# A fused two-stage attention kernel: the first key tile's exponentials move into the ring, the second stage's ring gets 12 places, and the planner's steps are replaced

## The reference

```python
x = x + tanh(g_xattn[0]) * xattn(layernorm(x), ctx_768, ...)   # softmax(q k^T / 8) v, 8 heads of 64; @ Wo + bo
x = x + tanh(g_ffn[0]) * ffn(layernorm(x), ...)
# ffn: q = (q / |q| + query_embedding) * softplus(temperature); softmax(q k^T / sqrt(32)) v, 16 heads of 32
#      gates = softmax(h @ Wr.T + br), top 3 of 15, times softmax(h @ Ws.T + bs); out = h * sum(gates) @ Wp.T + bp
```

## Time and profile before

| | us |
|---|---|
| median of 3 runs | 4596.27 (4593.71 to 4602.74) |
| profiled execution | 4595.59 |
| its span in the trace | 4593.8 |
| PE busy (matmuls) | 4350.3, 95% of the span |
| POOL busy | 3338.4, 73% |
| DVE busy | 2881.1, 63% |
| ACT busy | 2528.2, 55% |
| PE weight loads | 2348.5, 51% |

### The profile page before, as it was taken

How to read it: one execution, slowest core, us unless ns; L and a number is a source line. 1 busy time by engine, 2 the same in 40 slices (tenths; PEclk the granted TensorE clock), 3 DMA queues, 4 the chain that set the end, 5 groups by cost and what they waited for, 6 DMA issues and landing times.

```text
span 4593.8 us, 67810 instructions
## 1 busy us (share of the span) xinstructions
PE 4350.3 (95%) x21568; PEld 2348.5 (51%) x21568; DVE 2881.1 (63%) x3955; ACT 2528.2 (55%) x4641; POOL 3338.4 (73%) x2667
## 2 busy tenths in 40 slices
PE   4899999999999999999999999999999999999997
PEld 3455555555555555554445444544454454544443
DVE  4455656464646464676777767676777667677661
ACT  2353535454535454546666666567557666565664
POOL 1566666767666667558888878778788879677897
PEclk7899999999999999999999999999999999999999
DMA  7476766666656666653435345354443454362532
GB/s 230 129 194 173 205 173 197 178 194 182 182 168 184 174 177 175 169 147 104 136 106 173 90 136 154 83 155 117 124 143 103 124 152 106 112 181 70 146 109 83
DMA packets 516175, 682.26 MB, mean 149 GB/s; under 512 B 42736, under 2 KB 371952, under 8 KB 506608
## 3 DMA queue, kind: packets, MB, share of 16 engines
q1 hardware_dynamic: 515824, 677.92, 52.7%
HBM read 323.57 MB, written 150.99 MB: 103 GB/s over the span
## 4 chain that ended last, share of the span: by engine, by line
PE 80%; issue 8%; ACT 4%; DVE 4%; POOL 2%; DMA 2%; SPq 0%; ACTq 0%; POOLq 0%; DVEq 0%
PE aux L957 28%; PE aux L1049 19%; PE aux L1063 18%; PE aux L1031 7%; PE aux L1075 4%; DVE nm L1404 2%; ACT probs L1247 2%; PE aux L1001 1%; POOL added_f L936 1%; PE aux L1083 1%; PE aux L977 1%; POOL added L936 1%; ACT more L1247 1%; DMA xs<-in_x 1%; DMA v_kept<-v_out 0%
## 5 line engine op out<-in xcount | busy, mean ns | idle before, releaser
L936 POOL TENSOR_TENSOR added<-added,probs 128x512 f32<-128x512 f32 x1433 | 1792.0, 1289 | 773.7 <-PE aux L1063 620.7
L1404 DVE TENSOR_REDUCE nm<-aux 128x2 f32<-128x1024 f32 x1536 | 1810.9, 1220 | 581.9 <-PE aux L1031 581.4
L1247 ACT ACTIVATE probs<-aux 128x512 f32<-128x512 f32 x2151 | 1172.3, 603 | 876.1 <-PE aux L1049 740.0
L1049 PE MATMUL aux<-stack 128*128 128x512 f32 x4096 | 1323.0, 427 | 76.5 <-ACT probs L1247 36.5
L1049 PEld LDWEIGHTS aux<-stack 128*128 128x128 f32 x4096 | 711.4, 189 | 740.7 <-issue 284.0
L1063 PE MATMUL aux<-probs,v 128*32 128x512 f32 (+1 forms) x4302 | 934.5, 610 | 4.3 <-ACT probs L1247 2.3
L936 POOL TENSOR_TENSOR added_f<-added_f,probs 128x512 f32<-128x512 f32 x537 | 672.3, 1287 | 119.6 <-PE aux L1063 73.8
L957 PE MATMUL aux<-xT_hi,wqk 128*128 128x512 f32 x1536 | 560.4, 404 | 1.0 <-ACT more L1247 0.6
L1031 PE MATMUL aux<-ck_hi,cq_hi 32*128 32x512 f32 (+1 forms) x3072 | 453.9, 483 | 53.3 <-DVE nm L1404 35.8
L1031 PEld LDWEIGHTS aux<-ck_hi,cq_hi 32*128 32x128 f32 (+1 forms) x3072 | 181.0, 185 | 512.4 <-issue 511.0
L957 PE MATMUL aux<-wvo,parts 128*128 128x512 f32 x1536 | 400.2, 403 | 10.6 <-issue 10.2
(11 more groups left out here) (132 smaller groups left out, 4387.4 us busy)
## 6 DMA issues: line engine op xcount, KB each, us to landing
wqk<-w_split SPq DMA_DIRECT2D x256, 256.0 KB, 3.8
wvo<-w_split SPq DMA_DIRECT2D x64, 1024.0 KB, 7.2
parts<-h_kept SPq DMA_DIRECT2D x128, 512.0 KB, 3.9
stack<-cq_hi SPq DMA_DIRECT2D x128, 256.0 KB, 5.2
stack<-ck_hi SPq DMA_DIRECT2D x128, 256.0 KB, 5.5
v_kept<-v_out SPq DMA_DIRECT2D x128, 256.0 KB, 2.3
v<-v_kept SPq DMA_DIRECT2D x64, 512.0 KB, 4.4
h_kept<-h_hi SPq DMA_DIRECT2D x128, 256.0 KB, 2.8
```

What stands on the lines that cost most here:

```text
L936: pool.tensor_tensor(onto, onto, exp_buffer(T, e), ALU.add).then_inc(added_ok, 1)
L1049: ins = pe.matmul(out, stack[:, g % 2, e * ph.SLOTS + ks, jt * P:(jt + 1) * P], stack[:, g % 2, e * ph.SLOTS + qs, n * HALF:(n + 1) * HALF ...
L1247: act.activation(exp_buffer(T, e), aux[:, o.bank["S", T, e], :], ACT.Exp, scale=ph.SCALE).then_inc(probs_ok, 1)
L1404: dve.tensor_reduce(nm[:, half, first:first + 2 * TT - t:TT], aux[:, b:b + 2, :], axis=AX.X, op=ALU.max, negate=True).then_inc(emptied["dv ...
```

## The change

Four edits that go together.

- **First key tile.** All 8 key tiles of a half go through the ring. The sums get their own function, `sum_buffer`, on the same memory `added` and `added_f`. POOL's first addition of a half reads two exponentials (tiles 0 and 1) and writes the sum; it no longer waits for `PV`, but for the `sm` that read this sum buffer two halves ago. A ring place of tile 0 is free when tile 1 has been added (`added_by`). `ex` of tile 0, which waited for an `sm` two halves back, waits now as the other tiles do.
- **Ring.** The second stage's ring has 12 places (7 in `probs`, 5 in `more`); the first stage's stays at 7.
- **Memory.** The room comes from two buffers: the squares of the queries go into the place of the queries' low parts (`squares(n)`, one for each half, so that ACT waits for the copies of the group before it writes them), and the output bias of both stages lies in one tile `bo`, which a transfer `bi` and a scaling `bm` fill again between the stages.
- **Plan.** All numbers of `AT` are new, those of the second stage too, and the dependencies follow the edits above.

```diff
-        self.NP = 10 if ffn else 7
+        self.NP = 12 if ffn else 7
...
     def ring(self, T, e):
 
         t = T - TURN * self.first
-        return (t - t // TT - 1) * self.G + e
+        return t * self.G + e
 
     def ring_prior(self, T, e):
 
         m = self.ring(T, e) - self.NP
-        if T % TT == 0 or m < 0:
+        if m < 0:
             return None
         s, head = divmod(m, self.G)
-        return s + s // (TT - 1) + 1 + TURN * self.first, head
+        return s + TURN * self.first, head
+
+    def added_by(self, T, e):
+
+        return self.adds(T + (T % TT == 0), e)
...
-      dict(p=[3.46, 20.78, 34.23, 52.32], over=5.91, held=0.03, mx0=-6.14, mxn=10.85, ...
+      dict(p=[1.05, 21.66, 33.04, 50.6], over=5.54, held=0.1, mx0=-6.28, mxn=10.98, ...
...
+        self.add(("bi", 0), "sp", TURN * B + 50, [("xb", TT * B - 1)])
+        self.add(("bm", 0), "dve", TURN * B + 54, [("bi", 0)])
...
-            if T % TT == 0:
-                i = T // TT % 2 * ph.G + e
-                return added[:, i, :] if i < 4 else added_f[:, i - 4, :]
             i = ph.ring(T, e) % ph.NP
             return probs[:, i, :] if i < X.NP else more[:, i - X.NP, :]
 
+        def sum_buffer(h, e):
+
+            i = h % 2 * stage(h // HALVES).G + e
+            return added[:, i, :] if i < 4 else added_f[:, i - 4, :]
+
+        def squares(n):
+
+            return cq["lo"][:, n * HALF:(n + 1) * HALF].bitcast(F32)
...
                         if T % TT == 1:
-
-                            pool.wait_ge(weighed, T)
+                            if h >= 2:
+
+                                wait_full(pool, ("sm", h - 2), *([("sm", h - 1)] if h == HALVES * B else []))
+                            first = exp_buffer(T - 1, e)
                         else:
 
                             pool.wait_ge(added_ok, ph.adds(T - 1, e))
-                        pool.tensor_tensor(onto, onto, exp_buffer(T, e), ALU.add).then_inc(added_ok, 1)
+                            first = onto
+                        pool.tensor_tensor(onto, first, exp_buffer(T, e), ALU.add).then_inc(added_ok, 1)
...
-                        if (g, n) > (NG * B, 0):
-
-                            wait_emptied(act, ("ss", g, 0) if n else ("ss", g - 1, 1))
-                        act.activation(sq[:], src, ACT.Square, bias=bq[:, g % NG:g % NG + 1]).then_inc(sq_ok, 1)
+                        if n == 0:
+                            wait_stacked(act, g - 1, range(stage((g - 1) // NG).G))
+                        act.activation(squares(n), src, ACT.Square, bias=bq[:, g % NG:g % NG + 1]).then_inc(sq_ok, 1)
...
                             act.wait_ge(weighed, last + 1)
-                            if ph.is_added(last):
-                                act.wait_ge(added_ok, ph.adds(last, head))
+                            if last % TT < TT - ph.APART:
+                                act.wait_ge(added_ok, ph.added_by(last, head))
```

More of the change, by code:

```diff
@@ L577, in attention @@
         ones = sb("ones", [P, X.SUM])
-        bo_x = sb("bo_x", [P, DM])
+        bo = sb("bo", [P, DM])
         tg = sb("tg", [P, 2])
@@ L1000, in _ @@
                         pe.wait_ge(sq_ok, q_at["pqa", g, n])
-                        done(it, pe.matmul(out, blk[:], sq[:], start=True, stop=True))
+                        done(it, pe.matmul(out, blk[:], squares(n), start=True, stop=True))
                     elif kind == "vp":
@@ L1071, in _ @@
                         pe.wait_ge(added_ok, ph.adds(end - 1 - ph.APART, G - 1))
[L1072 to L1073 removed]
+                        if ph.APART:
+                            pe.wait_ge(probs_ok, ph.scores(end - 1, G - 1))
+                        for i in range(1 + ph.APART):
                             for e in range(G):
[L1075 removed]
+                                term = exp_buffer(end - i, e) if i else sum_buffer(h, e)
+                                ins = pe.matmul(out[e * D:(e + 1) * D, :], ones[:, 0:ph.SUM], term, start=i == 0, stop=i == ph.APART)
                         done(it, ins)
```

66 lines of the change are left out of this document (32 added, 34 removed), and 4 rows, old and new, of the table TAKES.

## The result

The kernel after takes 4469.32 us (median of 4 runs, 4468.38 to 4470.65), the kernel before beside it 4597.48 us. The ratio is 0.9726, with an interval of 0.9714 to 0.9737: 2.7% faster, 128 us.

A forecast was written before the change was run, and what follows sets the result against it. The prediction took the second stage to alternate between stretches bound by PE and by POOL, with too few buffers to average them. Terms -59 - 8 - 5 + 0 - 4 = -76 us from 4595.6 gave 4519 us, range 4480 to 4588.

The forecast's parts named there:

- PE has 0.5 us more to do than its busy mean: Second stage: PE's work in a batch is 303.4 us after the change, against a busy mean of 302.9 before.
- an idle time of 5.1: Batches 9 to 14: PE's idle time left in a batch, from 2.4, 1.7 and 1.0 us, giving batches of 308.5.
- the prices are 2.5% low: Batch 12 before: 294.4 us of PE's work counted against 301.8 busy, so counts were multiplied by 1.03.
- The rival called the floor: Rival, chance 0.13: POOL's earlier start removes nearly all PE idle time and matmuls flow without gaps; -115, 4480 us.
- The bound of 4471: Whole kernel, limit from below: all of PE's second-stage idle time and 10 us at the start go, 125 us.
- a half can't be shorter than that for long: Second stage: POOL's 24 additions of 1.29 us, 31.0 us, limit a half however little PE has to do.
- The rule that the prediction cites: Whole kernel: rule against the forecast; relieve the engine with highest occupancy, POOL, whose work doesn't change, so no gain.
- That wait goes: Second stage: POOL's first addition no longer waits for `PV`, so POOL enters each half up to 2.9 us earlier.
- 2.6 us that the ring lends: Middle of a second-stage half: with 12 places instead of 10, POOL may be 2.6 us later without being felt.
- POOL as the bound all along: Rival, chance 0.08: POOL's work is unchanged, so a wait removed on it turns into another; 4595 to 4600 us.
- The loss at the start of a half: Rival 'Slower', chance 0.09: the first tile's exponentials wait at a half's start; +62 or +31, 4627 us.
- Waits for ACT in the fourth half: Rival 'Half of the gain', chance 0.15: idle time returns as waits for ACT, bunched in the fourth half; 4560 us.

The follow-up runs named there:

- ring11: The kernel after with 11 places instead of 12 in the second stage, sequence planned anew for 11: 4580.71 us, ratio 0.9973.
- light additions: POOL's second-stage additions of key tiles 2 to 6 on half of the columns: 4573.13 us in the kernel before, 4461.03 us in the kernel after.
- old_steps1: The kernel after with the first stage's planner steps (first dict of AT) from before: 4600.39 us, ratio 1.0018.
- both light engines: Exponentials (batches 9 to 15) and POOL's second-stage additions, key tiles 2 and later, on half of the columns: 4548.93 us in before, 4446.42 us in after.
- old_steps: The kernel after with both dicts of AT from before, so the new structure with an order planned from the old steps: 4612.77 us, ratio 1.0039.

## Why the prediction was wrong in size

**The mechanism, as far as it held.** PE's work is spread by the new order as counted, the light halves go but for the fifth, and batches 9 to 14 are alike. That the spread is what brings the gain did not hold as I wrote it: ring11 is as even by the count and takes 320.8 us a batch, and the new steps with 10 places are more even than before and slower. The prediction took the evenness from after's finished order, and what else that order does right came with it unnamed: it leaves PE 19 gaps in a batch, where before has 42 on average and ring11 32 to 34 in batches 12 and 13. The halves of batch 12 come out at 40.8, 36.6, 35.6, 36.6, 29.5, 45.6, 34.1 and 45.0 us, for counts of 36.8, 37.9, 35.3, 36.5, 25.9, 43.7, 33.1 and 44.8. The first stage stayed at its time, with 236.2 to 236.5 us in five of batches 1 to 6. Batch 5 takes 240.8, which is over the bound of 238 that I set; light additions in after show such a batch at another place (batch 4), so it doesn't belong to the order.

**The step that failed: PE's busy time was taken as its work.** The prediction said "PE has 0.5 us more to do than its busy mean", 303.4 us in a batch; that is why even an idle time of 5.1 gave only 308.5. With 1,652 matmuls in batch 12 of either kernel, the busy time fell to 296.7, and to 296.8 in the mean of three. This term alone is 6 x 6.6 = 40 us too high. Idle time was forecast at 5.1 and is 7.0, 6 x 1.9 = 11 us the other way; the two make 28 to 29 of the 29.4 us by which batches 9 to 14 miss. What lies in the 6.1 us between the busy means 302.9 and 296.8 can be worked out from the list of matmuls. PE has 36, 41 and 48 gaps in batches 12 to 14 before (idle times of any length) and 19, 19 and 18 after. In before the matmul after a gap adds 0.50 us of busy time on average, where the same kinds add 0.33 in the flow; in after it is 0.52 and 0.38. That makes 41.7 x 0.17 - 18.7 x 0.14 = 4.5 us. Another 1.1 is the granted clock, below; 0.5 stays unexplained. So by this estimate a gap costs its idle time and 0.15 to 0.2 us that the profile books as busy. The counts had shown it: busy time lies 7.4, 8.6 and 11.8 us over the count in batches 12 to 14 before, with 36, 41 and 48 gaps, and 2.7 in after with 19. The prediction read the first three as "the prices are 2.5% low" and carried them over as work. The Trainium skill, Perfetto Trace Analysis, section Identifying the Most-Contended Engine, says that matmul busy time is no good measure of how close PE is to its limit, since pipelined matmuls look smaller in the trace. I had quoted the first half of this and then added up busy time all the same. The trace agrees that busy time is not work, though here it is larger than the counted work, and larger the more gaps there are. The rival called the floor had this mechanism ("matmuls that now wait between exponentials flow without gaps") and its 4480 is the nearest of my times; I gave it 0.13. The bound of 4471 from "PE's idle time only" was no bound.

**The step that was wrong without showing in the sum: POOL as the pace.** I wrote that "a half can't be shorter than that for long", 31.0 us, and took POOL's being busy in each of 31.4 us as the proof. With POOL's additions light the half takes 30.6. Nor are 31.0 us a floor for a half: the half of `old_steps1` above takes 26.1 with whole additions, and the profile of the kernel before has one of 29.7, the fifth of batch 13, which the prediction does not use. POOL was busy all the time because the half was about as long as its work for other reasons too: by the timeline, round trips of score and exponential with nothing of PE's between them. The rule that the prediction cites, from the Trainium skill, Perfetto Trace Analysis, section Identifying the Most-Contended Engine (relieve the engine with the highest occupancy, PE judged by its weight loads), would have pointed to POOL and is no better: halving most of its additions gains 0.4%. What fits is the section Optimization Strategy of that page of the Trainium skill, on kernels with several regimes, which may gain when these are interleaved; the new order does that, though ring11, as even by the count, gains nothing in batches 9 to 14. The same section of the Trainium skill takes repeated gaps on the engine that should be busy as a possible lack of buffers. Here two more places without the order gave nothing (4636 against 4632 us), and one less with it cost 93.

**The terms for the first addition and for the ring.** "That wait goes" was right, the 68.8 us of the earlier trace rows are gone. That it frees POOL by 2.9 us in a half was not: POOL now waits for exponentials instead (28.8 + 28.6 + 14.7 + 14.4 = 86.5 us in the two rows of after above and the two for `more`; 47.8 in before), and is waited for only 0.8 us. The ring's "2.6 us that the ring lends" to POOL had the wrong borrower, the lead of the scores. No step of my sum said that the order depends on 12 places, where 11 cost 81 of the 88 us.

**Smaller terms.** Batch 7 gave 10.6 us where I took 0: the first stage was counted only for its steady batches, and in batch 7 PE has 27 matmuls less in the new order, some 4 us at my prices; its busy time falls by 7.4 and its idle time by 3.3. Batch 0 gave 5.2 us although PE has 19 matmuls more there, some 3.4 us: idle time falls from 16.4 to 9.1 us and the loss by the clock (below) from 11.9 to 5.1. The start (-2.1 against -4) was nearly right. Batch 8 (-8.9 against -8) was right by luck: its terms (321.3 less 17.9 idle, plus 1.5 of work) reach "about 313" only with 8 us left idle that I gave no reason for; 12.7 were idle, and the busy time was 3.7 lower where 1.5 more had been counted. Batch 15 with the tail (-10.1 against -5) was too low; its idle time is 31.7 us against 38.6. Light additions gain 13 us in before's batch 15, so POOL is felt there, where I took nothing for it. These and the 29.4 us make the miss: 29.4 + 10.6 + 5.2 + 5.1 + 0.9 - 1.9 - 0.5 = 48.8 us, against the profiled execution.

**The other rivals.** POOL as the bound all along is refuted by its light additions. The loss at the start of a half did not come, though POOL has little room: with the wait for `PV` kept the kernel loses 338 us. Waits for ACT in the fourth half are small: it takes 36.6 us, and 35.8 with exponentials and additions light, where the prediction had 1.0 for them.

**What stays open.** Of before's light half of 31.4 us, 25.6 are counted; both light engines together took 1.9. That the remaining 3.9 are gaps for want of PE's other work is argued from the timeline; no run filled them. What in after's order leaves PE so few gaps is known only in part: the count of work by halves does not tell it, and DVE's maxima close together are one likely cost of the other orders. Before's own order with the new buffers wasn't tried (the kernel `old_steps` has an order planned anew), nor more than 12 places. Of the runs with the whole computation none is faster than the kernel after.

## What to carry to other kernels

An engine that is busy for all of a stretch need not be its pace: lighten it in one run before you build on it. Busy time of PE holds what its gaps cost, here 0.15 to 0.2 us for each, so a forecast should add up counted work and the price of the gaps (294 us counted in a batch, 303.8 measured) and not start from the busy time. Work that is spread evenly by the count is no forecast either: two orders with nearly the same spread took 303.8 and 320.8 us. Where an order comes from a planner, resources and steps are one change: the structure alone lost 0.4%, the second stage's steps alone 1%, together they gained 2.7%, and the test of any part has to hold the finished order fixed.

## What the runs showed of the hardware

The clock grant adds to the price of waits. Three windows of the kernel before (columns as above), two neighbouring ones first:

```profile
3950.00:3960.00 10.00, 8.30 (x54) 2.93 (x51) 7.71 (x9) 6.57 (x13) 3.80 (x4) 1.00 0.75 206
3960.00:3970.00 10.00, 9.75 (x54) 3.80 (x54) 5.81 (x24) 5.96 (x13) 7.93 (x7) 0.83 0.94 229
3980.00:3990.00 10.00, 10.00 (x48) 4.48 (x44) 6.99 (x6) 5.44 (x11) 10.00 (x9) 0.83 0.01 2
```

In the second, behind a window in which PE was busy 8.3 of 10 us, the granted clock is 0.83: for a part of the window it is at the lower of its two levels (0.50, 1.2 GHz), for the rest at the upper one. In the third it is 0.83 as well, and PE shows as fully busy (10.00 of 10.00): the busy share doesn't show the lower clock. Summed as (1 - granted clock) x length, the time lost in batches 9 to 14 is 8.5 us in before, 1.7 in after, 31 with 12 places planned and 11 run, 34 in ring11 and 84 in the order for 10 places with 12. Over the whole kernel it is 71 us before and 47 after. By this estimate, which takes PE as bound by its clock in that time, some 7 of the 88 us in these batches came back through the clock, and of the 103 us between ring11 and after in these batches 32 are clock; no term of the prediction had it.
